# A two-layer decoder on one core: which jobs run while batch 1's mix is made, and how the last attention begins

## The reference

```
x = x + L0_attn(ln(x))     # below
x = x + L0_xattn(ln(x), ctx)   # one head of 128, then Wo
x = x + L0_ffn(ln(x))      # 2 shared + top-2 of 8 gelu experts
x = x + L1_attn(ln(x))     # 16 heads, everything fake-quantised to 8 bits
x = x + L1_xattn(ln(x), ctx)   # 16 heads of 8, then a relu MLP
x = x + L1_ffn(ln(x))      # 1 shared + top-2 of 16 gated experts
```

```
ctx    = softmax(mod * q k^T / sqrt(8)) v                # "gated", 16 heads of 8
ctx    = 0.3 ctx + 0.7 (mha_4heads(h, h) Wout_c + b)     # "causal", no mask in fact
ctx    = 0.85 ctx + 0.15 (mha_4heads(ctx, ctx) Wout_m + b)  # "meta", q, k, v from the mixed ctx
out    = ctx @ Wo + bo
```

## Time and profile before

| | us |
|---|---|
| median of 3 runs | 669.84 (668.92 to 670.2) |
| the profiled execution | 669.52 |
| its span in the trace | 667.8 |

### The profile page before, as it was taken

How to read it: one execution, slowest core, us unless ns; L and a number is a source line. 1 busy time by engine, 2 the same in 40 slices (tenths; PEclk the granted TensorE clock), 3 DMA queues, 4 the chain that set the end, 5 groups by cost and what they waited for, 6 DMA issues and landing times. The chain is left out here.

```text
span 667.8 us, 9519 instructions
## 1 busy us (share of the span) xinstructions
PE 588.5 (88%) x3347; PEld 325.6 (49%) x3347; DVE 416.6 (62%) x868; ACT 383.8 (57%) x686; POOL 91.4 (14%) x98
## 2 busy tenths in 40 slices
PE   8388899989999788999999999388888958998997
PEld 7022233222334445889998995112222325645886
DVE  6677776668722734645654227879999256746774
ACT  4167776767765246757664441346989733686631
POOL 7111100110001000800000000399000030000000
PEclk9689999999999579999999996659999977999999
DMA  6362200731073200200000000000000001100000
GB/s 176 82 80 39 73 1 2 95 69 30 1 316 62 34 1 9 116 1 1 1 1 1 15 3 0 0 0 2 2 2 2 1 1 56 45 4 1 0 17 17
DMA packets 14978, 22.69 MB, mean 34 GB/s; under 512 B 3716, under 2 KB 10100, under 8 KB 14548
## 3 DMA queue, kind: packets, MB, share of 16 engines
q1 hardware_dynamic: 13108, 15.54, 10.9%
q10 hardware_dynamic: 1824, 6.55, 2.7%
HBM read 9.99 MB, written 0.52 MB: 16 GB/s over the span
## 5 line engine op out<-in xcount | busy, mean ns | idle before, releaser
L536 DVE TENSOR_REDUCE negmax<-ps 128x2 f32<-128x1024 f32 x96 | 114.2, 1220 | 36.5 <-PE ps L467 36.1
L583 ACT ACTIVATE probs<-ps 128x512 f32<-128x512 f32 x192 | 105.8, 598 | 37.8 <-PE ps L486 36.1
L583 ACT ACTIVATE probs_q<-ps,score_scale 128x512 f32<-128x512 f32 x128 | 78.2, 687 | 15.9 <-PE ps L486 14.5
L1964 PEld LDWEIGHTS ps<-experts,hid 128*128 128x128 f32 x640 | 82.6, 191 | 6.9 <-issue 1.0
L1964 PE MATMUL ps<-experts,hid 128*128 128x128 f32 x640 | 84.0, 275 | 0.0
L536 DVE TENSOR_REDUCE negmax_q<-ps 128x2 f32<-128x1024 f32 x64 | 74.9, 1218 | 6.6 <-PE ps L467 5.9
L2040 ACT ACTIVATE hid<-ps 128x512 f32<-128x512 f32 x80 | 46.7, 598 | 45.6 <-PE ps L896 45.5
L896 PE MATMUL ps<-experts,wfc 128*128 128x512 f32 x156 | 49.3, 424 | 0.0
L467 PE MATMUL ps<-gated 64*128 64x512 bf16 x128 | 28.3, 419 | 19.2 <-DMA gated<-parts 7.9
L2134 DVE SCALAR_TENSOR_TENSOR x_tok<-ps,comb,x_tok 128x128 f32<-128x128 f32 x64 | 18.0, 343 | 43.2 <-PE ps L1964 43.2
L486 PE MATMUL ps<-quantised 32*128 32x512 bf16 x128 | 38.4, 405 | 3.2 <-ACT probs_q L583 1.0
(11 more groups left out here) (396 smaller groups left out, 958.2 us busy)
## 6 DMA issues: line engine op xcount, KB each, us to landing
experts<-in_L_ffn_Wfc_dram ACTq DMA_DIRECT2D x1, 2560.0 KB, 10.1
experts<-in_L_ffn_Wproj_dram ACTq DMA_DIRECT2D x1, 2560.0 KB, 16.0
gated<-parts SPq DMA_DIRECT2D x18, 128.0 KB, 2.5
q_wide<-parts SPq DMA_DIRECT2D x6, 256.0 KB, 5.7
k_wide<-parts SPq DMA_DIRECT2D x6, 256.0 KB, 7.6
q_wide<-parts SPq DMA_DIRECT2D x12, 128.0 KB, 3.6
k_wide<-parts SPq DMA_DIRECT2D x12, 128.0 KB, 3.5
qs_x<-crossing SPq DMA_DIRECT2D x5, 256.0 KB, 2.9
```

The lines of the kernel that those rows point to most:

```text
L536: nc.vector.tensor_reduce(maxima, scores, AX.X, ALU.max, negate=True).then_inc(self.a_max_done, 1)
L583: nc.scalar.activation(self.probs[0:size, g % self.P_SLOTS, :], ps[0:size, self.B_BANK + g % self.B_SLOTS, :], ACT.Exp, scale=scale).then_ ...
L1964: last = nc.tensor.matmul(K.ps[:, y_bank(g), i * P:(i + 1) * P], hid[:, m % SLOTS, i * P:(i + 1) * P], wproj[:, FT * e + f, :], start=(f = ...
```

## The change

**Order of the jobs.** Batch 0's meta jobs become 11 and 12, batch 1's causal jobs 13 and 14; `held` stays 15. `D 0` runs as extras at units 169, 171 and 173, where `C 1` and P 17 to 19 stood. `C 1`, P 17 to 19, the loads `H`, and the cross attention's steps up to SCORES run between job 14's turn and job 15's first A block, with fillers; the steps from PROBS to RAW stand between the 8 A blocks. What was among the B and V steps (PROBS, VALUES, OUT, STATS2) and behind them (TURN2, LOW, RAW) is gone from there, apart from FIRST, which splits the first expert's weights.

**The last attention's beginning.** Minimum and maximum of all tokens but the last job's 32 columns of batch 1 are taken at unit 122 of the quantised attention (`N`), the last 32 columns at the end; the bias is added behind `out_second`. The q projection is one matmul on columns of Wq that POOL has put in the jobs' order beforehand (with one more small matmul and one more ACT copy for the bias, in the experts' block). Each load of X.q is two, of 64 source partitions each, the first three for jobs 0 and 1 of a batch, the others (`stacked_late`) for jobs 2 and 3. POOL's constants wait for layer norm 4. `keep_busy` behind `spread_range` gives 4 fillers in place of 6.

```diff
+    MIXED = {("C", 0): 1, ("D", 0): 2, ("C", 1): 3}
@@ tensor steps
-                pe.wait_ge(self.c_ready, self.stk.items[b]["meta"] + 1)
+                pe.wait_ge(self.c_ready, self.MIXED["C", self.stk.items[b]["meta"]])
...
-            pe.wait_ge(self.c_ready, NB + b + 1)
+            pe.wait_ge(self.c_ready, self.MIXED["D", b])
@@ scalar steps
-            if i == WideCross.NORM:
+            if i in (WideCross.NORM, WideCross.STATS2):
                 self.K.nc.scalar.activation(self.K.warm[:, :], self.K.eps[:, :], ACT.Exp)
@@ jobs
         jobs += jobs_of("gated", b, (7 * b, 7 * b + 2, 7 * b + 3))
+        if b:
+            jobs += jobs_of("meta", 0, (14, 15, 16))
         jobs += jobs_of("causal", b, (7 * b + 4, 7 * b + 5, 7 * b + 6))
-    for b in range(NB):
-        jobs += jobs_of("meta", b, (14 + 3 * b, 15 + 3 * b, 16 + 3 * b))
+    jobs += jobs_of("meta", 1, (17, 18, 19))
@@ extras
-    for at, step in ((168, ("C", 1, 0)), (170, ("C", 1, 1)), (170, ("C", 1, 2)), (172, ("P", 17, 0)),
-                     (173, ("P", 18, 0)), (175, ("P", 19, 0))):
+    for at, step in ((169, ("D", 0, 0)), (171, ("D", 0, 1)), (173, ("D", 0, 2))):
...
-    extras["held", held] = [("H", 17, 0), ("D", 0, 0)]
...
+    extras["held", held] = [("K", 3, 6), ("C", 1, 0), ("X", 0, X.NORM), ("C", 1, 1), ("C", 1, 2), ("X", 0, X.NORMED),
+                            ("K", 5, 6), ("P", 17, 0), ("P", 18, 0), ("H", 17, 0), ("X", 0, X.TURN), ("P", 19, 0),
+                            ("X", 0, X.Q), ("K", 2, 6), ("X", 0, X.SCORES), ("K", 7, 6)]
+    extras["after", ("A", held, 0)] = [("X", 0, X.PROBS)]
...
-    extras["end"] += [("K", 4, 7), ("W", 1, 0), ("K", 4, 7)]
+    extras["end"] += [("K", 2, 7), ("W", 1, 0)]
@@ CrossTiles
+        pe.wait_ge(self.n["spread"], 4)
+        nc.tensor.matmul(K.ps[:, bank, 192:193], self.by_jobs[:, 1, :], self.q_bias_given, start=True, stop=True,
...
+    def spread_weights(self, pool, weights):
+
+        for i, w in enumerate((weights, self.K.ident)):
+            for f in range(2):
+                self.K.nc.gpsimd.tensor_copy(
+                    self.by_jobs[:, i, 64 * f:64 * (f + 1)].rearrange("p (s d g) -> p s d g", s=4, g=2),
...
@@ QuantOutputs
+    def ends_of(self, at, tokens):
+        nc, chain, t = self.K.nc, self.chain, slice(at * TPB, (at + 1) * TPB)
+        chain(nc.vector.tensor_reduce(self.ends[:, 0, t], tokens, AX.X, ALU.min, negate=True))
+        chain(nc.vector.tensor_reduce(self.ends[:, 1, t], tokens, AX.X, ALU.max))
+    def first_ends(self, dve, sem, value):
+        dve.wait_ge(sem, value)
+        self.ends_of(0, self.tok_a[:, 0:TPB, :])
+        self.ends_of(1, self.tok_a[:, TPB:NT, 0:self.LAST])
...
     def find_range(self, dve):
         dve.wait_ge(*self.tokens_done)
-        self.range.reduce(chain, flat).then_inc(self.spread.reduced, 1)
-        for b in range(NB):
-            nc.vector.tensor_tensor(tiles, tiles, self.row["L1_attn_proj_b"]...
+        self.ends_of(2, self.tok_a[:, TPB:NT, self.LAST:D])
+        nc.vector.tensor_reduce(self.range.tile[:, 0:2, 0], self.ends[:, :, :], AX.X, ALU.max) \
@@ last attention
-                interleaved(nc, K.ps[:, 4 + b, :], W["L1_xattn_Wq"], K.h_ft[:, half(b)], STRIP_SIDES) \
+                nc.tensor.matmul(K.ps[:, 4 + b, :], X.by_jobs[:, 0, :], K.h_ft[:, half(b)], start=True, stop=True) \
...
-            load(sp, 0, (0, 2))
-            load(sp, 1, (0, 1, 2))
+            load(sp, 0, 0, (0, 2))
+            load(sp, 0, 1, (0, 2))
+            load(sp, 1, 0, (0, 1, 2))
+            load(sp, 1, 1, (0, 1, 2))
...
+            pool.wait_ge(ln.xn_ready, NT)
             ready.make(nc.gpsimd, pool)
...
             outputs.out_second(dve)
+            outputs.add_bias(dve)
```

More of the change, by code:

```diff
@@ L1033, in decoder_kernel @@
         Q = QuantTiles(K, sb)
[L1034 removed]
+        X = CrossTiles(K, sb, W, row, y_ft, columns_sb)
         with ExitStack() as st:
@@ L1359, in gated_attention @@
     X = WideCross
-    extras["held", held] = [("H", 17, 0), ("D", 0, 0)]
[L1361 to L1367, removed]
+    extras["after", ("E", held - 1, 0)] = [("K", 2, 6)]
+    extras["held", held] = [("K", 3, 6), ("C", 1, 0), ("X", 0, X.NORM), ("C", 1, 1), ("C", 1, 2), ("X", 0, X.NORMED),
+                            ("K", 5, 6), ("P", 17, 0), ("P", 18, 0), ("H", 17, 0), ("X", 0, X.TURN), ("P", 19, 0),
+                            ("X", 0, X.Q), ("K", 2, 6), ("X", 0, X.SCORES), ("K", 7, 6)]
+    extras["after", ("A", held, 0)] = [("X", 0, X.PROBS)]
+    extras["after", ("A", held, 1)] = [("X", 0, X.VALUES)]
+    extras["after", ("A", held, 2)] = [("X", 0, X.OUT)]
+    extras["after", ("A", held, 3)] = [("X", 0, X.STATS2)]
+    extras["after", ("A", held + 1, 1)] = [("X", 0, X.TURN2)]
+    extras["after", ("A", held + 1, 2)] = [("X", 0, X.LOW), ("X", 0, X.RAW)]
+    extras["after", ("A", held + 1, 3)] = [("K", 3, 6)]
     extras["end"] = [("D", 1, 0)]
@@ L1372, in gated_attention @@
     extras.setdefault(100, []).append(("X", 0, X.KV))
[L1373 to L1376, removed]
-    extras["end"] += [("K", 4, 7), ("W", 1, 0), ("K", 4, 7)]
+    extras.setdefault(180, []).append(("X", 0, X.FIRST))
+    extras["after", ("E", len(jobs) - 1, 0)] = [("S", 0, 0)]
+    extras["end"] += [("K", 2, 7), ("W", 1, 0)]
     prologue[2:2] = [("Q", 0, 0)]
@@ L1816, in __init__ @@
         self.parts = sb("parts_kx", [P, 2, keys], F32R)
-        self.n = {x: K.sem("kx_" + x) for x in ("made", "projected", "full", "first", "second", "v_out", "stacked")}
+        self.by_jobs, self.q_bias = sb("weights_by_jobs", [P, 2, P]), sb("bias_by_jobs", [P, 1])
+        self.n = {x: K.sem("kx_" + x) for x in ("made", "projected", "full", "first", "second", "v_out", "stacked", "spread")}
     def bias(self, name):
@@ L2279, with extra_vector @@
     lead_growth = 4
+    def extra_vector(self, dve, step):
+        if step[0] == "N":
+            self.outputs.first_ends(dve, *self.free_at["T", step[1], 0][1])
 class Spread:
@@ L2312, with __init__ @@
 class QuantOutputs:
-    def __init__(self, K, row, Q, tok_a, ft_a, o_ints, out_range, spread_out, n, chain, tokens_done):
+    LAST = 96
+    def __init__(self, K, row, Q, tok_a, ft_a, o_ints, out_range, spread_out, n, chain, tokens_done, ends):
+        self.ends = ends
         self.K, self.row, self.Q, self.tok_a, self.ft_a, self.o_ints = K, row, Q, tok_a, ft_a, o_ints
@@ L2713, in cross_attention_heads @@
     mparts = sb("mparts_x", [TPB * 4, 5, 2, P], F32R, st)
-    s = {k: [K.sem(f"x1_{k}{b}") for b in range(NB)] for k in ("projected", "high", "low", "stacked")}
-    bias = X.bias("L1_xattn_bq")
+    s = {k: [K.sem(f"x1_{k}{b}") for b in range(NB)] for k in ("projected", "high", "low", "stacked", "stacked_late")}
+    bias = X.q_bias[:, :]
     jobs = [CrossJob(X.q, X.k, X.v, 32, list(range(g, g + 4)), 8, b, [(0, NK)], b * S, b * CTX_PAD, tok_a, 8.0 ** -0.5,
@@ L2735, in low_part, with load @@
             .then_inc(s["low"][b], 1)
-    def load(eng, b, which):
+    def load(eng, b, side, which):
+        rows = slice(64 * side, 64 * (side + 1))
         for c in which:
@@ L2740, in load @@
             eng.wait_ge(s[("high", "low")[part]][b], 1)
-            eng.dma_start(as_f32(X.q[c::4, :, half(b)]), as_f32((q_high, q_low)[part][:, half(b)])) \
-                .then_inc(s["stacked"][b], 16)
+            eng.dma_start(as_f32(X.q[c::4, 2 * side:2 * side + 2, half(b)]), as_f32((q_high, q_low)[part][rows, half(b)])) \
+                .then_inc(s[("stacked", "stacked_late")[side]][b], 16)
     with nc.Block() as block:
```

36 lines of the change are left out of this document (24 added, 12 removed).

## The result

| | us |
|---|---|
| before, median of 4 | 670.02 (668.92 to 671.47) |
| after, its four runs | 675.02, 677.30, 691.23, 698.48 |
| ratio without the two longest | 1.009, 95% interval 1.0046 to 1.0134 |
| the profiled execution after | 691.23 (span 689.2, mean clock 0.898) |

By its two shorter runs the changed kernel is 0.9% slower, where no change was forecast and 670.8 predicted. So there are two results to explain: some 6 us over before in the shorter runs, and 15 to 22 us more in the longer. The profiled execution is of the longer kind; its first block and its last part are read as they are, and the longer kind's cost lies apart in the quantised attention. E9's profile, of a shorter run, is read beside it.

The account below looks back on a forecast made before the run. PE was taken to bound the stretch before job 14's end; DVE, PE's half clock and waits the held stage. First block +4.2, experts +0.2, range -3.4, POOL +0.3, stacks -0.3 gave 670.8 against 669.84; range 665 to 675.5.

Parts of the forecast that it names:

- the wait: First block, job 14's last V to job 15's first A: 15.7 us instead of 2.8, range 14.7 to 17.8.
- V's end: First block, end of job 14's last V: 2.65 us earlier, less 0.2 for a wait of D 0.
- rival B: First block: PE's clock falls in the wait, +3, and the held A stage another +1 to +2; 675 us, chance 0.20.
- B and V, tail: End of the first block: first B to last V 14.7 us instead of 21.0, then 4.8 instead of 7.0 to the experts.
- The A blocks: First block, first A to first B of job 15: 20.8 us instead of 18.8, with 16.5 DVE work and 4.3 idle.
- The last part: Range stretch ahead of the last attention's first A: -3.4 us, range -4.1 to -2.5.
- Reductions: Range: two reductions of 1.22 us become two over an eighth of the elements plus a small one, -1.6 us.
- waiting for the bias adds: Range: L2305 no longer waits for the two bias adds after PE's turn is done, -1.85 us.
- adds put back: Range: the two bias adds return behind out_second, 2 x 0.68 us, where DVE idles 0.77: +0.6 us.
- The two projections: Last attention's q projection: eight strip matmuls become one matmul, 0 us, range -0.5 to +0.9.
- the first A's wait for its stacks: Last attention's beginning: halved transfers, with jobs 0 and 1 waiting for first halves only, -0.3 us, range -1.0 to 0.
- Rival D: Last attention: SP's ten issues delay L615's first issue until some 2 us after it is due; 672.8 us, chance 0.08.

Follow-up runs that it names:

- E9: The changed kernel again, unedited: six runs of 677.65, 678.41, 691.50, 691.69, 699.17 and 699.74 us.
- E6: The changed kernel with 26 more filler matmuls in PE's waits of the A stage: 670.66 us, ratio to before 1.0008.
- E2: The kernel before with all of the change except the first block's hunks: median 668.12 us, ratio 0.9961.
- E3: The kernel before with 34 more filler matmuls at the end of the first block: median 684.4 us.
- E7: The kernel before with 17 more filler matmuls at the end of the first block: median 677.4 us.
- E12: The kernel before with 68 more filler matmuls at the end of the first block: median 687.9 us.
- E5: The changed kernel with one filler matmul ahead of each of 40 B steps in the quantised attention: 690.77 us.

## Why the prediction was wrong

*Order of the stages and the wait: right.* 16.2 against 15.7: the last transfer that job 15 needs was issued 12.1 behind V's end (12.2 forecast), and the first A came 4.1 behind that issue where 3.5 was forecast. PE's clock stayed full in it, so the slower rival B failed as it was put (below 1 from 5 us behind V's end). That its 675 is the nearest of all to the shorter runs is luck.

*B and V, tail: right.* 14.8 and 4.9 against 14.7 and 4.8: what a stage saves when steps leave it could be read from the rows of before.

*V's end: mis-sized by 0.5.* -1.9 against -2.45.

*The A blocks: the step that failed in the first block.* The sum has 16.5 us of DVE work and 4.3 of idle there and no term for a fall of the clock; the text put such a fall, as rival B, into the wait, with +1 to +2 for the A stage behind it. The fall came behind the wait, where PE was busy 2.04 of 4 us at 232; in the wait, with its chain and fillers, it had been busy 2.5 to 3.7 of 4. 23.9 instead of 20.8 in the longer run and 23.0 in E9's shorter one; E6 gives 19.7 with the clock up. That term, with the 0.5 and 0.5 above, makes the first block +8.4 and +7.3 for +4.2. E6 is the kernel that the forecast describes: its first block is 3.7 longer than before's (forecast 4.2), and it takes 670.66. That this meets the 670.8 to 0.1 is luck: in its span a start later by 1.3 stands against a last part of -4.0.

*The last part: right in size, with two terms off that cancel.* -4.2 against -3.4 in the longer run, -3.8 in E9. Reductions -1.7 (-1.6), waiting for the bias adds -1.85 (-1.85), L2306 -0.6 (-0.6), adds put back +0.85 (+0.6), small steps around them -0.3 (none), POOL's work beside L2775 and the maxima 0 (+0.3; L2775 takes 0.75 with POOL's select beside it and L2733 0.75 without). The two projections gave -0.4 and -0.9 (0 forecast; the second ran in before at a clock of 0.54 to 0.61 from 560 to 568 and in after at 1.00), and the first A's wait for its stacks gave +0.6 (-0.3 forecast). Rival D came in kind but not in size: L615 waited 0.28 for SP's queue and not some 2. The first A waited for the halved stacks (1.16 idle, ended by the transfer); whole transfers were not tried in this place. The page of after gives the ten transfers of 128 KB a median of 2.9 us to landing, before's five of 256 KB also 2.9 (section 6 of the page), so halving brought no sooner landing. The Trainium skill ("SBUF — State Buffer", "Can I just issue two DMAs to hit both halves?") had said that only a transfer over all 128 partitions reaches all ports and that two half ones serialise; the trace agrees in the time, and does not show the ports.

*Not in the prediction at all: what runs behind the first block.* The sum has no term for the 300 us of unchanged code between the two changes, nor for what follows the second. In the longer run this was +15.6 in the quantised attention. In E9's shorter run it was nothing there, but +2.5 in the last attention, where the clock fell once more (it did in E2 too), and 2.5 came from a later start ahead of all changed code. The quantised attention took 122.8 to 139.7 us from its first maxima row to the projection's stacks, in kernels with the same instructions there. Delays of the unchanged kernel made it longer (E3 and E7; hardly in E12), fillers there kept the clock up (E5), and the unedited kernel gave 124.5 and 139.7 from the same start. What in the chip makes one start good and another bad stays open; so does why the same kernel gets either from run to run.

*The chances.* From their parts they add up to faster 0.32, same 0.26 and slower 0.42, not 0.34, 0.25 and 0.41; nothing hangs on it.
